# The feed-forward part of a transformer block as one interleaved row of 32 chunks, with a pre-summed LayerNorm a group ahead

## What is computed

```
ada = cond @ ada_w + ada_b ; shift1, scale1, gate1, shift2, scale2, gate2 = split(ada)
x1  = ln(x) * (1 + scale1) + shift1                  # L0: transformer block, 16 heads of 128
a   = softmax(q k^T / sqrt(128)) v @ out_w + out_b
y   = x + gate1 * a
h   = gelu((ln(y) * (1 + scale2) + shift2) @ ffn_w1 + ffn_b1)     # 256 -> 1024
x   = x + y + gate2 * (h @ ffn_w2 + ffn_b2)                       # 1024 -> 256
x   = x + gru(x, start = cond)                       # L1: 32 steps in turn
x   = x + pooled_attention_norm(x)                   # L2
x   = x + rk4_oscillator(x, start = cond)            # L3: 32 steps in turn
```

## Time and profile before

| | us |
|---|---|
| median of 3 runs (981.15 to 983.85) | 982.87 |
| the profiled execution | 982.24 |
| its span, first to last instruction | 980.5 |
| attention, up to the last sum of the unit before the last | 478.9 |
| last attention unit and feed-forward part | 478.9 to 613.6 |
| from the last matmul down to the first input gate | 613.6 to 620.9 |
| input gates | 620.9 to 631.1 |
| GRU, pooling, oscillator | 631.1 to 980.5 |

### The profile page before, as it was taken

One profiled execution on the slowest core, in us unless ns is written; L12 is line 12 of the kernel. 1 busy time (PEld: TensorE's weight loads), 2 busy tenths in 40 slices (PEclk: granted clock), 3 DMA queues, 4 the chain that ended last, 5 costly groups with the idle time before them and its releaser, 6 DMA issues.

```text
span 980.5 us, 18799 instructions
## 1 busy us (share of the span) xinstructions
PE 932.5 (95%) x7278; PEld 776.8 (79%) x7278; DVE 606.4 (62%) x1685; ACT 422.7 (43%) x1149; POOL 248.6 (25%) x343
## 2 busy tenths in 40 slices
PE   7999999999999999999988989699999799999998
PEld 6787887888877888777755657599987399999997
DVE  5545445464455544446464454577777978888887
ACT  3233322233223322223373554355545556666665
POOL 0644400020000100001005433333313643334432
PEclk9999999999999999999999999899999989999999
DMA  7122000000000000000240000000000000000000
GB/s 283 55 87 77 1 1 1 1 1 1 2 1 1 1 1 1 1 2 1 87 182 1 0 0 0 1 2 1 1 2 2 1 1 2 23 2 23 4 20 23
DMA packets 5429, 21.98 MB, mean 22 GB/s; under 512 B 608, under 2 KB 736, under 8 KB 4960
## 3 DMA queue, kind: packets, MB, share of 16 engines
q1 hardware_dynamic: 5344, 20.82, 5.9%
HBM read 18.72 MB, written 2.10 MB: 21 GB/s over the span
## 4 chain that ended last, share of the span: by engine, by line
PE 78%; issue 9%; DVE 6%; ACT 3%; POOL 3%; POOLq 0%; DVEq 0%; ACTq 0%
PE ps L324 36%; PE ps L668 7%; PE ps L672 6%; PE ps L538 6%; PE ps L388 6%; PE ps L667 5%; PE ps L528 4%; PE ps L540 2%; PE ps L377 2%; PE ps L331 2%; DVE BD L1076 1%; PE ps L545 1%; POOL fc L1504 1%; POOL ysc L1542 1%; POOL fc L1509 0%
## 5 line engine op out<-in xcount | busy, mean ns | idle before, releaser
L1046 DVE SCALAR_TENSOR_TENSOR o_lo<-ps,vec,o_hi 128x512 fp32r<-128x512 f32 x64 | 48.1, 751 | 111.9 <-ACT o_hi L752 111.9
L324 PE MATMUL ps<-x_hi,W_hi 128*128 128x512 f32 x256 | 108.7, 425 | 4.9 <-DVE x_lo L1139 2.7
L736 ACT ACTIVATE qk<-ps,vec 128x512 f32<-128x512 f32 x64 | 44.0, 688 | 136.1 <-PE ps L324 136.1
L324 PE MATMUL ps<-x_lo,W_hi 128*128 128x512 f32 x256 | 100.7, 393 | 0.0
L324 PE MATMUL ps<-x_hi,W_lo 128*128 128x512 f32 x256 | 100.6, 393 | 0.0
L668 PE MATMUL ps<-rk_th,cpc 128*128 128x128 f32 x512 | 99.3, 296 | 1.3 <-ACT rk_th L984 1.1
L1504 POOL TENSOR_TENSOR xc<-xc,rs 128x1024 f32<-128x1024 f32 x4 | 10.0, 2502 | 339.6 <-DVE rs L1025 201.4
L752 ACT ACTIVATE o_hi<-ps,vec 128x512 fp32r<-128x512 f32 x64 | 44.0, 688 | 117.4 <-PE ps L388 117.4
L1035 DVE TENSOR_SCALAR qk<-ps,vec 128x512 f32<-128x512 f32 x64 | 47.5, 742 | 73.6 <-PE ps L324 73.6
L668 PEld LDWEIGHTS ps<-rk_th,cpc 128*128 128x128 f32 x512 | 73.3, 193 | 9.9 <-ACT rk_th L984 7.6
L667 PE MATMUL ps<-rk_th,cpc 128*128 128x64 f32 x512 | 79.4, 258 | 0.0
(11 more groups left out here) (250 smaller groups left out, 2200.3 us busy)
## 6 DMA issues: line engine op xcount, KB each, us to landing
stage<-qkv_w SPq DMA_DIRECT2D x6, 768.0 KB, 4.3
stage<-out_w SPq DMA_DIRECT2D x4, 512.0 KB, 3.8
f_raw<-ffn_w SPq DMA_DIRECT2D x2, 1024.0 KB, 6.0
xorig<-xT SPq DMA_DIRECT2D x1, 2048.0 KB, 8.0
out<-xtb SPq DMA_DIRECT2D x4, 512.0 KB, 3.1
x_all<-xT SPq DMA_DIRECT2D x1, 1536.0 KB, 14.0
ada_sb<-ada_w SPq DMA_DIRECT2D x1, 1024.0 KB, 9.8
BD<-qkv_w SPq DMA_DIRECT2D x1, 768.0 KB, 6.3
```

The costliest lines, as they stand in the source:

```text
L324: r = pe.matmul(out_, lhsT, rhs, start=first and i == 0, stop=last and i == n - 1)
L736: act.activation(qk[:, 0, h % 2, :], ps[:, PJ[0], :], ACT.Identity, bias=col("qkv_b", HU * u + h)).then_inc(act_evac, 1)
L1046: dve.scalar_tensor_tensor(o_lo[:, h % 2, :], ps[:, OB[h % 2], :], col("qkv_b", 2 * HEADS + HU * u + h), o_hi[:, h % 2, :].bitcast(F32), A ...
```

## The change

Everything from the last attention unit to the first step of the GRU is put in another order.

- **Statistics.** For the first LayerNorm of groups 2 and 3 and for the whole second LayerNorm, POOL adds the two halves first (`sum_inputs`, `sum_squares`), and PE makes one matmul with `ones` (`stat_of_sum`) where it made two. The second LayerNorm begins one unit earlier for group 0; its first steps for group 1 come into the last attention group; for groups 2 and 3 each step is one group ahead, and VectorE (`l2_norm`, `l2_scale`, `l2_shift`) does there what POOL did. `m_hi` and `m_lo` have two buffers each.
- **Weights.** `ffn_w1` and `ffn_w2` are fetched after units 12 and 13 are projected, two or three units earlier, and POOL splits them (`ffn_high`, `ffn_low`, 128x2048 each).
- **The row of chunks.** `up(k)` and `down(k)` for k = 0 to 31. Chunks 0 to 3 go up inside the last attention unit (list `LAST`). Then `up(k)` and `down(k - 2)` alternate. `up` uses three banks in turn, `down` adds each chunk into two banks that change with the group (`ACC`). The three-round loops are gone.
- **The end.** POOL adds the attention result to the block's input beforehand (`with_input`), so one addition for each half is left in `finish`. After the last matmul down VectorE gates the first eight time rows of the last sixteen sequences on their own (128x128), adds and splits them; POOL has split the other sequences' first rows already (`split_old`). PE does the state matmuls of step 0 ahead of the input gates, and step 0's operations are put between the six copies of `gi` (order `FIRST_GATES`). The Sigmoid table is loaded after the last Gelu. Four small preparations for the oscillator move into GRU steps 1 to 4.

```diff
+FIRST_GATES = (0, 1, 2, 4, 3, 5)
+SUMS1 = NG - 2
+LAG = 2
+        UP = (PJ[0], PJ[1], SB)
+        ACC = (OB, YB, OB, PJ)
+        def up_bank(k):
+            return UP[k % 3] if k < MC * (NG - 1) else (*YB, SB)[k % 3]
...
-            sp.wait_ge(proj_done, 12 * NU * NG)
+            n = NU * (NG - 1) + 1
+            sp.wait_ge(proj_done, 12 * n)
             sp.dma_start(f1_raw[:, :, :], ffn_w1).then_inc(ld_ffn[0], 16)
+            sp.wait_ge(proj_done, 12 * (n + 1))
             sp.dma_start(f2_raw[:, :, :], ffn_w2).then_inc(ld_ffn[1], 16)
...
+            def stat_of_sum(src, s):
+                pe.matmul(ps[:, TB, :], ones[:, :], src, start=True, stop=True).then_inc(s, 1)
...
+            LAST = [("L", 1), ("U", 0), ("U", 1), ("PV", 0), ("PV", 1), ("U", 2), ("Y", 0), ("PV", 2), ("Y", 1), ("PV", 3),
+                    ("U", 3), ("Y", 2), ("Y", 3)]
...
+            def up(k):
+                g, m = k // MC, k % MC
+                if m == 0:
+                    pe.wait_ge(m_lo_s, KC * (g + 1))
...
+                if k >= 3:
+                    pe.wait_ge(gel_done, 2 * (k - 2))
...
+            def down(k):
+                g, m = k // MC, k % MC
+                pe.wait_ge(glo_done, k + 1)
...
+            down(0)
+            down(1)
+            for k in range(4, MC * NG):
+                g, m = k // MC, k % MC
+                up(k)
+                if m == 4 and g + 2 < NG:
+                    l2_mean(g + 2)
+                if m == 1 and 0 < g < NG - 1:
+                    l2_var(g + 1)
+                down(k - LAG)
+            for k in range(MC * NG - LAG, MC * NG):
+                down(k)
...
+                if t == 0:
+                    pe.wait_ge(iw_lo, 1)
+                    input_gates(0, 0, 36)
...
-            pe.wait_ge(iw_lo, 1)
-            input_gates(0, 0, 36)
             pe.wait_ge(h0, 1)
+            pe.wait_ge(gel_done, 2 * MC * NG)
```

More of the change, by code:

```diff
@@ new lines, in down @@
+            def down(k):
+                g, m = k // MC, k % MC
+                pe.wait_ge(glo_done, k + 1)
+                if k == 0:
+                    pe.wait_ge(fw_2, 2)
+                    pe.wait_ge(olo_done, 1 + HEADS * NG)
+                if k == MC:
+                    pe.wait_ge(gate_done, 1 + len(GATE) * NG)
+                if k == 2 * MC:
+                    pe.wait_ge(fgate, KC)
+                if k == 3 * MC:
+                    pe.wait_ge(gel_done, 2 * (k - 1))
+                for c in range(KC):
+                    cs = slice(c * P, c * P + P)
+                    r = three(ps[:, ACC[g][c], :], [(f2_hi[:, m, cs], f2_lo[:, m, cs], g_hi[:, m, :], g_lo[:, m, :])],
+                              first=m == 0, last=m == MC - 1)
+                    if m == MC - 1:
+                        r.then_inc(acc_done, 1)
+                if m < MC - 1:
+                    r.then_inc(down_done, 1)
@@ L810, in attention @@
                         high(g + 1)
+                    if u == 0 and last:
+                        l2_square(0)
                     if u == 1 and last:
-                        l2_square(0)
+                        l2_sqrt(0)
                     if u == 2 and last:
-                        l2_sqrt(0)
-                    if u == NU - 1 and last:
                         m_high(0)
-                    if project:
-                        query(n, un, 2)
+                    if not project:
+                        break
@@ L829, in _ @@
             for g in range(NG):
                 attention(g, g == NG - 1)
-            def ffn(g, last):
-                for m in range(MC):
-                    act.wait_ge(up_done, MC * g + m + 1)
-                    act.wait_ge(glo_done, 1 + MC * g + max(m - 1, 0))
-                    act.activation(gel[:, m % 2, :], ps[:, PJ[m % 2], :], ACT.Gelu,
-                                   bias=col("ffn_b1", m)).then_inc(gel_done, 1)
-                    act.wait_ge(down_done, 1 + KC * g)
-                    act.activation(g_hi[:, m, :], ps[:, PJ[m % 2], :], ACT.Gelu,
-                                   bias=col("ffn_b1", m)).then_inc(gel_done, 1)
-                    if m == 1 and not last:
-                        l2_square(g + 1)
-                    if m == 5 and not last:
-                        l2_sqrt(g + 1)
-                if not last:
-                    m_high(g + 1)
@@ L1167, in attention @@
                         low(g + 1)
+                    if u == 0 and last:
+                        l2_center(0)
                     if u == 1 and last:
[L1169 removed]
+                        l2_recip(0)
                     if u == 2 and last:
[L1171 to L1173 removed]
+                        m_low(0)
+                        l2_center(1)
+                    if not project:
+                        break
@@ L1226, in _ @@
[L1226 to L1232 removed]
+            last_unit()
@@ L1557, in split_inputs @@
+            with_input(1)
+            l2_sum_squares(3)
+            with_input(2)
+            finish(1)
+            with_input(3)
+            finish(2)
+            split_old()
+            finish(NG - 1, 8)
             def split_inputs(j):
```

522 lines of the change are left out of this document (334 added, 188 removed).

## The result

| | before | changed |
|---|---|---|
| median, us | 982.02 (981.15 to 983.85, 4 runs) | 935.46 (935.23 to 936.9, 4 runs) |
| profiled execution, and its span | 982.24, 980.5 | 935.23, 933.5 |
| PE busy, share of the span | 95% | 97% |
| ratio | | 0.9525, 95% interval 0.9507 to 0.9543 |

The prediction was 937, from 931 to 948. No run shows why; it is left out, and that kernel was profiled a second time.

A forecast was written before the change was run, and what follows sets the result against it. PE was taken to bound the kernel: only less PE work helps in attention, waits and low clock cost time later. Savings 10.2 + 25.8 + 9.3 = 45.3 us from 982.2 gave 937 us, range 931 to 948.

The forecast's parts named there:

- Part 1: Statistics summed on POOL: twelve matmuls with `ones` go, at 0.855 us each, saving 10.2 us.
- Part 2: Last attention unit and row of chunks: of 28.3 us loss all but 2.5 goes, saving 25.8 us.
- 2.5 were kept: New loss in last unit and row: 0.4 us in the unit, 1 for short gaps, 1 for holds.
- 6.4 us of short gaps: Last unit and row before: gaps too short to show as idle, blamed on ACT emptying one of two banks.
- Part 3: From last matmul down to GRU step 1: 22.5 us become 13.2, saving 9.3; bounds 5 and 10.3.
- margin of 0.3: Allowance of 0.3 us within the 13.2 us expected from last matmul down to GRU step 1.
- Part 4: GRU preparations, earlier transfers and POOL's 128x2048 instructions: no effect on the time.
- (a): Row of chunks: VectorE and POOL share the bound, four to eight holds cost 5 to 11 us; 942 to 948; chance 0.20.
- slack of 3.4 us: Row of chunks: a `g_lo` may come 3.4 us late without cost to PE.
- (b): Attention: late softmax delays the transposes, about 941, or removed statistics do not shorten the units; chance 0.08.
- (c): Row of chunks: brief pauses drop PE's clock, 0.20 us more per matmul, 1014 us if all are slow; chance 0.03.
- (d): Row of chunks: a count one too strict keeps pairs in step and the gaps remain; about 950 us; chance 0.03.

The follow-up runs named there:

- the gates first: Changed kernel with the 36 input gates of GRU step 0 put back ahead of its state matmuls; 938.18 us, ratio 0.956.
- the four moves: Changed kernel with later attention gate, group 1's first LayerNorm summed on POOL, feed-forward gate at chunk 5, POOL's last additions behind `y_lo`; 933.55 us, ratio 0.9502.

## Where the prediction was right and where it was wrong

**Part 1, predicted 10.2.** Mis-sized. The price of a matmul was right. "Six are in attention units, where PE is never idle, so they count in full" fails in both halves. Five fewer stand in the attention stretch, seven in the row, and the stretch got 3.2 us shorter and not 5 x 0.855 = 4.3: the two matmuls of a mean had covered a gate that stands ahead of a key, and one covers only half of it. That costs a wait of 1.01 us at each of three places, where the kernel before had 1.91 at one, 0.15 at another and none at the third. The row of 395.87 was in the trace of before, and shows what happens where no mean stands at that place; I had read a unit without it (421 to 450) for all. With the full price for the seven in the row, part 1 comes to 3.2 + 6.0 = 9.2. That price is assumed there: doubled in the changed kernel, the five that are left cost the row 2.8 of 4.3 us, and all twelve 6 of 10.3.

**Part 2, predicted 25.8.** Right. The last unit and the row lost 31.80 us, less 7 x 0.855 = 6.0 for statistics, leaves 25.8. That it fits to the tenth is luck, since the 6.0 is assumed. The work left there is 87.2 + 5.4 + 3.6 + 5 x 0.855 = 100.5 of 102.64 us, so 2.1 us are loss where 2.5 were kept. Of its reasons, one fell: the 6.4 us of short gaps were put down to the two banks. In the old order a third bank shortened the stretches by only 2.7 us, and the loops account for nothing in the row. No run takes the other 3.7 apart; behind waits the matmuls start further apart for a while, which is the likely place. The depth of two chunks carries 8 us of the part, the filled last unit 2.8; the third bank nothing. The other 15 us were not tested one by one: the waits of before for `fsq` (5.7) and `f_lo` (2.2), the larger part of those for `g_lo` and the low clock are gone from the trace, with statistics a group ahead, the earlier weights and the alternation all in the change together.

**Part 3, predicted 9.3.** Right: 9.1. The small operations before `y_lo` took some 3.0 us and not 2.2 (that is PE's wait with the gates first), so 0.4 were left behind the state matmuls, near the margin of 0.3. The 0.4 is a hold by POOL, which the prediction had only in its bound: the two `y_lo` take 1.30 us here and 0.49 in the four moves, where POOL is held back until they are done. VectorE, then POOL:

```profile
578.34 1.30 DVE L1385 TENSOR_TENSOR y_lo<-xtb,y_hi 128x128 fp32r<-128x128 f32 x2
```

```profile
578.29 1.01 POOL L1747 TENSOR_TENSOR xtb<-ysc,xorig 128x384 f32<-128x384 f32 x1 [3.68 <-DVE ysc L1370]
```

In the four moves PE's wait is gone.

**Part 4, predicted nothing.** The rest of the kernel took 1.0 us less, which is within what the part behind the row moves from run to run (2 us in one of the experiments, at a lower clock in the pooling part).

**The sum, 45.3,** against 47.0 of the two spans, or 45.1 without the different start: 9.2 + 25.8 + 9.1 + 1.0. That part 4 gave the 1.0 us that part 1 lacked is luck. The landmarks came where they were expected: the last matmul down at 576.48 (near 578), step 1's state matmuls at 590.14 (near 591).

**The rivals.** (a) was seen at its place, four subtractions in 6.55 us, and took 1.0 us of PE and not 5 to 11. The slack of 3.4 us swallowed the rest, in group 1 by little. The prediction read the 3.39 us of the earlier trace rows a little wrong: not the first but the second `g_lo` was held, and its end at 518.91 is 0.55 behind POOL's at 518.36, as in the pairs above. (b) fell: no wait for `BD`, and removed statistics did shorten the units. (c) fell: the clock is 1.00 in all stretches from 300 to 650 us. The rule on accumulations that cycle through PSUM banks, in the Trainium skill's "TensorE: Matmul & The Clock Gate", "A second HAM failure mode: psum-queue depth-cycling", did not bite here, with a change of bank every six matmuls; what the page tells of is another kernel, in bf16. (d) fell: chunks up and down alternate 1.36 us apart.

## What to carry to other kernels

When work is taken from the busiest engine, look at who used that time as cover: the same place in a round where that work does not stand (here a group boundary without a mean) shows in the trace of before what is late next. Of two stages of a pipeline that alternate on one engine, the distance can matter more than another buffer: here one step closer cost 8 us, and a third bank gave nothing. And a step moved on one engine moves the steps that it releases on another, so read that one's order as well before counting the gain.

## What was not expected of the hardware

- VectorE's two subtractions of 128x512 took 5.19 us beside two POOL additions that followed each other without a pause, and 3.49 us beside one; alone they take about 1.3. The waiting VectorE got its turn between the two additions: its first subtraction ended at 527.08, 0.55 us behind the first addition. VectorE's `scalar_tensor_tensor` with one operand in PSUM kept its 0.70 to 0.75 us.
- Behind a wait of 0.7 or 1.0 us the matmuls ran at a granted clock of 1.00, and still each wait cost some 0.1 to 0.3 us more than it showed (the three for `qk` 0.25 each): six matmuls of 128x512 took 1.49 us behind the wait at 551.74 us, and 1.36 elsewhere. Not every wait went by at full clock: behind the one of 1.97 us in the four moves the clock was 0.70 over 5 us, behind the one of 1.91 at 395.87 us in the kernel before the matmuls started 0.23 us apart.
